# Softmax shares multiplied into the probability rows in place, in the attention stream of a four-layer kernel

## The reference

```
scores = einsum('bhqd,bhkd->bhqk', q, k) / sqrt(32)      # k, v: image key first, then 512 words
scores = where(kj <= qi + 1, scores, -10000.0) + mask
attn = softmax(scores, axis=-1)
out = einsum('bhqk,bhkd->bhqd', attn, v).transpose(0, 2, 1, 3).reshape(B, S, 512) @ c_proj_w + c_proj_b
x = x + out
```

## Time and profile before

| | |
|---|---|
| median of 3 runs | 4083.1 us (4080.97 to 4084.29) |
| the profiled execution, its own time | 4085.57 us |
| its span in the trace | 4083.9 us |
| TensorE busy | 3902.9 us (96%) |
| VectorE busy | 2336.8 us (57%) |
| ScalarE busy | 1064.0 us (26%) |
| attention stream | from 3059 us of the span to its end |

### The profile page before, as it was taken

How to read it: one execution, slowest core, us unless ns; L and a number is a source line. 1 busy time by engine, 2 the same in 40 slices (tenths; PEclk the granted TensorE clock), 3 DMA queues, 4 the chain that set the end, 5 groups by cost and what they waited for, 6 DMA issues and landing times. The chain is left out here.

```text
span 4083.9 us, 170825 instructions
## 1 busy us (share of the span) xinstructions
PE 3902.9 (96%) x77684; PEld 2648.1 (65%) x77684; DVE 2336.8 (57%) x8378; ACT 1064.0 (26%) x3931; POOL 158.9 (4%) x373
## 2 busy tenths in 40 slices
PE   6799999999999999999999999998679999999998
PEld 4577777777666666678887777765435555555555
DVE  3565655666566566556556655665326656666564
ACT  1111111111111111111111111111005555555554
POOL 0000000000000000000000000000000000000000
PEclk9999999999999999999999999999969999999999
DMA  5000000000000000000000000001000000000000
GB/s 187 3 4 4 3 3 3 3 4 3 3 3 3 4 3 3 3 4 3 3 4 3 3 3 3 3 3 64 2 6 1 14 11 9 11 12 14 11 6 19
DMA packets 34256, 46.75 MB, mean 11 GB/s; under 512 B 5820, under 2 KB 22252, under 8 KB 33527
## 3 DMA queue, kind: packets, MB, share of 16 engines
q1 hardware_dynamic: 31222, 29.43, 2.3%
q10 hardware_dynamic: 2304, 6.29, 0.4%
HBM read 27.33 MB, written 8.39 MB: 9 GB/s over the span
## 5 line engine op out<-in xcount | busy, mean ns | idle before, releaser
L201 PE MATMUL bank<-wh,h 128*16 128x256 f32 (+1 forms) x17408 | 1002.7, 370 | 52.6 <-ACT h L237 50.8
L181 PE MATMUL bank<-wh,h 128*8 128x256 f32 x16384 | 991.0, 381 | 62.2 <-DVE h L356 31.3
L201 PEld LDWEIGHTS bank<-wh,h 128*16 128x16 f32 (+1 forms) x17408 | 540.1, 97 | 333.9 <-ACT h L237 75.6
L181 PEld LDWEIGHTS bank<-wh,h 128*8 128x8 f32 x16384 | 482.4, 90 | 379.0 <-DVE h L356 50.2
L328 DVE STREAM_TRANSPOSE tp<-bank 128x256 f32<-128x256 f32 x512 | 230.4, 450 | 644.1 <-PE bank L181 644.1
L187 PE MATMUL bank<-wh,h 128*8 128x128 f32 x16384 | 550.9, 274 | 0.0
L187 PEld LDWEIGHTS bank<-wh,h 128*8 128x8 f32 x16384 | 455.6, 90 | 106.2 <-issue 2.5
L250 ACT ACTIVATE gates_sb<-pre_sb 128x32 f32<-128x32 f32 x512 | 117.5, 230 | 1357.6 <-DVE pre_sb L330 1357.6
L225 PE MATMUL bank<-stage,w_qkv 128*32 128x128 f32 x11904 | 386.4, 273 | 0.0
L225 PEld LDWEIGHTS bank<-stage,w_qkv 128*32 128x32 f32 x11904 | 344.3, 110 | 42.6
L237 ACT ACTIVATE h<-sum 128x64 f32<-128x64 f32 (+1 forms) x544 | 137.8, 253 | 786.9 <-DVE sum L272 786.9
(11 more groups left out here) (131 smaller groups left out, 3346.8 us busy)
## 6 DMA issues: line engine op xcount, KB each, us to landing
xrows<-in_x_dram SPq DMA_DIRECT2D x32, 256.0 KB, 3.8
out_dram<-X SPq DMA_DIRECT2D x32, 256.0 KB, 2.6
w_qkv<-in_L_cond_c_attn_w_dram SPq DMA_DIRECT2D x1, 3072.0 KB, 17.7
wh<-in_L_cond_w_W_dram ACTq DMA_DIRECT2D x4, 512.0 KB, 8.5
w_qkv<-in_L_cond_w_W_dram ACTq DMA_DIRECT2D x4, 512.0 KB, 10.3
wx<-in_L_cond_Wx_dram SPq DMA_DIRECT2D x2, 1024.0 KB, 8.3
wh<-in_L_cond_Wh_dram SPq DMA_DIRECT2D x2, 1024.0 KB, 10.5
mask_all<-in_mask_Bx1x1xS_ff_dram SPq DMA_DIRECT2D x8, 256.0 KB, 3.3
```

The lines of the kernel that those rows point to most:

```text
L181: mm = pe.matmul(mem.ps0[32 * j:32 * j + B, 0:2 * P], h0[:, us, k, ts, :], columns_of(mem.wh0[:, k, 0:3:2, :], j), start=(k == 0), stop=(k ...
L201: mm = pe.matmul(mem.ps12[32 * j:32 * j + B * len(ls), P * l0:P * l1], h12[:, us, k, ts, l0:l1, :].rearrange("p l b -> p (l b)"), columns_ ...
```

## The change

The probability rows themselves are multiplied by their share, in place, by VectorE, before TensorE turns them. `shares` has one number for each row and head (it was spread to 128 columns). The extras (image and hidden weights) are multiplied by the share too. TensorE no longer turns the shares, ScalarE no longer copies them, and VectorE copies bank 7 where it multiplied it. A new signal, `probs_ready`, stands between VectorE's last multiplication and TensorE's first transpose of the unit.

```diff
                     if r <= qc:
                         if r == 0:
-                            pe.wait_ge(s.exps_done, HPG * (v + 1))
+                            pe.wait_ge(s.probs_ready, v + 1)
...
                     else:
-                        pe.wait_ge(s.sums_ready, v + 1)
-                        pe.wait_ge(s.extras_in, v + 1)
-                        pe.transpose(bank[:, P:2 * P], mem.shares[:, v % RING, :], mem.ident[:, :])
                         mm = pe.matmul(bank[FAR * qc:FAR * qc + EXTRAS * HPG, 0:P],
...
-                        if qc == 0 and v >= 2 * QC:
-                            act.wait_ge(s.weighed_kept, v // QC - 1)
                         rows = slice(FAR * qc, FAR * qc + EXTRAS * HPG)
-                        nc.scalar.copy(mem.probs_extra[rows, :], bank[rows, 0:P])
...
-                        nc.scalar.copy(mem.shareT[:, v // QC % 2, qc * P:(qc + 1) * P],
-                                       bank[:, P:2 * P]).then_inc(s.turn_kept, 1)
+                        nc.scalar.copy(mem.probs_extra[rows, :], bank[rows, 0:P]).then_inc(s.turn_kept, 1)
...
                 dve.wait_ge(s.sums_full, i + 1)
-                nc.vector.reciprocal(mem.shares[:, slot, :].rearrange("p (g c) -> p g c", g=HPG),
-                                     mem.sums[:, slot, :].unsqueeze(2).to_broadcast([P, HPG, HD])).then_inc(s.sums_ready, 1)
+                nc.vector.reciprocal(mem.shares[:, slot, :], mem.sums[:, slot, :]).then_inc(s.sums_ready, 1)
+                dve.wait_ge(s.sums_ready, i + 1)
+                dve.wait_ge(s.extras_in, i + 1)
+                nc.vector.tensor_tensor(mem.extras[:, slot, :].rearrange("p (g e) -> p g e", e=EXTRAS),
+                                        mem.extras[:, slot, :].rearrange("p (g e) -> p g e", e=EXTRAS),
+                                        mem.shares[:, slot, :].unsqueeze(2).to_broadcast([P, HPG, EXTRAS]), ALU.mult)
+                for g in range(HPG):
+                    row = mem.probs[qc][:, g, 1:]
+                    ins = nc.vector.tensor_scalar(row, row, mem.shares[:, slot, g:g + 1], None, ALU.mult)
+                ins.then_inc(s.probs_ready, 1)
...
                     dve.wait_ge(s.weighed, i - 2)
-                    dve.wait_ge(s.turn_kept, ended[i - 2])
-                    nc.vector.tensor_tensor(mem.attnT[hg // HG % 2][:, hg % HG, :], mem.banks[7][:, :],
-                                            mem.shareT[:, hg % 2, :], ALU.mult).then_inc(s.weighed_kept, 1)
+                    nc.vector.tensor_copy(mem.attnT[hg // HG % 2][:, hg % HG, :], mem.banks[7][:, :]).then_inc(s.weighed_kept, 1)
...
-        mem.shares = sb(ctx, "shares", [P, RING, P])
-        mem.shareT = sb(ctx, "shareT", [P, 2, T])
+        mem.shares = sb(ctx, "shares", [P, RING, HPG])
```

More of the change, by code:

```diff
@@ L1135, in __init__ @@
         self.sums_ready = new("sums_ready")
+        self.probs_ready = new("probs_ready")
         self.weighed = new("weighed")
```

## The result

The changed kernel takes 4164.73 us (median of 4 runs, 4162.82 to 4172.67) against 4082.03 us before in the same comparison: ratio 1.0204, interval 1.0188 to 1.0220, slower by 83 us. The forecast was 4148 us with a range of 4106 to 4197.

The account below looks back on a forecast made before the run. TensorE was taken to bound the kernel, busy 198.56 of 200 us. Terms -30 + 14 + 16 + 33 + 20 + 12 = +65 us gave a median of 4148 us, 8-in-10 range 4106 to 4197.

Parts of the forecast that it names:

- Bound and mechanism: TensorE bounds the stream; its first transposes would wait for VectorE's sums and multiplications, which stand behind a kept product.
- The removal: On TensorE, 128 transposes of the shares at 0.235 us each go: -30 us.
- I read 0.195 as 0.067 plus 0.13 fixed: VectorE's in-place multiplications: 0.195 us apart at 128 columns, 0.067 for columns plus 0.13 fixed; 0.395 at 512.
- full length: Rival: VectorE's multiplication runs at 1.04 ns a column, 0.60 us at 512; +117 us, 4200 us; chance 0.13.
- no surcharge: Rival: VectorE's multiplication issues at 0.01 us plus half a ns a column; +21 us, 4104 us; chance 0.08.
- errata table: Skill-page estimate for VectorE's multiplication: 58 cycles and half the columns at 0.96 GHz, 0.33 us for 512; sum +47 us.
- The chain: Time from start of `sums_of` to release of TensorE's first transpose: 2.28 us for qc = 3, 2.02 for qc = 2.
- the release of TensorE: Time taken for releasing TensorE behind VectorE's multiplications: 0.08 us.
- The stalls: TensorE's waits before first transposes: 0.62 us 23 times, 2.35 us 7 times, 1.22 us 27 times, plus 20 us at the ends.
- jobless steps: About 12 steps of first and last sequence without a job between; stalls of 1.3 to 2.3 us each, 20 us.
- The clock: Granted clock dips after the 7 longest TensorE stalls, 1.7 us lost each: 12 us; none charged to shorter stalls.
- The clock rival: Rival: TensorE stalls of 1.22 us also bring a clock dip, 46 us more, 4194 us; chance 0.12.

Follow-up runs that it names:

- the load alone: Changed kernel with multiplications writing to a spare tile, TensorE turning unmultiplied rows once the exponentials are done; 4060.23 us against 4080.6 for the kernel before.
- the removals alone: Changed kernel without the extras' and rows' multiplications and without the wait for them; 4055.41 us against 4080.6 for the kernel before.

## Why the prediction was right, and what was mis-sized

**Bound and mechanism.** Right. TensorE bounds the stream, and `probs_ready` stands behind a kept product. A wait there costs 31 us even without the new work, the load alone nothing measurable.

**The removal.** -30 us forecast, -25 to -27 measured (3.40 us a sequence). At `l % 4 = 3` it gave 0.37 and not 0.26 us, as the rows of before (weigh, shares, extras) and after show:

```profile
4000.74 0.43 PE L813 MATMUL bank<-probsT,v 128*32 128x128 f32 x8
4001.09 0.33 PE L789 MATMUL bank<-ident,shares 128*128 128x128 f32 x1
4001.36 0.39 PE L790 MATMUL bank<-ident,extras 128*8 128x128 f32 x2
```

```profile
3727.57 0.43 PE L810 MATMUL bank<-probsT,v 128*32 128x128 f32 x8
3727.82 0.38 PE L787 MATMUL bank<-ident,extras 128*8 128x128 f32 x2
```

From L813 to the extras 4001.36 - 4000.74 = 0.62 us before, 0.25 after. TensorE thus arrives sooner at that wait, which makes the wait longer and the step no shorter. Elsewhere it gave less: the steps of the run with the removals alone are shorter by 0.11 us at `l % 4` = 0 and 2, 0.25 at 1 and 0.37 at 3. The distance from one start to the next, from which the term was taken, was a fair mean and wrong for each place.

**The price of a multiplication.** The step "I read 0.195 as 0.067 plus 0.13 fixed" held: from 281 ns at 128 columns the length grows by 0.52 ns a column, and four of 512 take 1.67 us, (1.67 - 0.48) / 3 = 0.397 from one to the next for a forecast 0.395. The rivals of full length and of no surcharge fall with it. The Trainium skill, page "VectorE: DVE Perf Modes", section "The perf-mode tier table", has the two elements a cycle that this slope shows; the estimate of 0.33 us for 512 columns by its errata table was short by 0.07. With a constant for the scalar it is (1.43 - 0.42) / 3 = 0.337 us, so what the figure lacked here is the price of the scalar from a row. The 0.13 us fixed are thus 0.06 for the scalar, as the rows of L919 and L922 had it, and 0.07 that the multiplications have with a constant too.

**The chain.** 2.28 and 2.02 us forecast, 2.36 and 2.09 measured. It is the release of TensorE that was too short: at `l = 11` the multiplications end at 3564.54 + 1.40 = 3565.94, and the transposes start 0.14 us later, for 0.08 taken.

**The stalls.** 83 us forecast, 90.4 measured as waits. At `l % 4 = 3` 1.22 forecast, 1.33 to 1.40 measured (0.07 from the chain, 0.11 from the larger removal); at `l` = 4, 8, 12 0.62 against 2.36 - (1.87 - 0.11) = 0.60, with 0.53 shown as a wait, where an error of 0.08 in the chain and one of 0.10 in the removal cancel; at `l = 0` 2.35 against 2.36 to 2.43. The places of `l % 4 = 3` are 28 and not 27. Waits of 1.33, 0.53 and 2.36 us at 28, 23 and 7 places are 66 us; the other 24 us, where 20 was forecast, stand in ten waits at the start of the stream and in the jobless steps. An even sequence comes to 6.28 us where the sum had 4 x 1.22 + 3 x 0.62 + 2.35 - 3.76 = 5.3.

**The clock** was the term most off. I charged 12 us to the seven `l = 0` waits. The windows give instead, as length times what lies under the clock of before, about 813 x 0.02 = 16 us in the middle and 172 x 0.10 = 17 in the last sequence of the profiled execution; of the latter some 12 show in the length, since TensorE's busy time rose there by 147.10 - 138.87 = 8.2 us though about 3.4 of work went; the rest must have fallen into waits.

Dips came at steps of several kinds, and not at every `l = 0`. The clock rival (a dip at each 1.2 us wait) did not hold either: of the 24 waits of 1.33 us in the six middle sequences five have a dip behind them. Filling the waits took 22 us off and these five dips away, which puts them down to the idle TensorE; the run with a constant, which waits 1.09 us at the same places, has none there. For the dips at `l` = 1 and 2 that is not shown, and why five of 24 waits bring one stays open; the places are counted in one profiled execution of each kernel. The median execution is 8 us shorter than the profiled one, with a mean granted clock of 0.977 for 0.974, so it should hold fewer dips.

In all, 83 us is 18 over the forecast sum: some 8 from waits, 3 to 5 from the smaller removal, the rest, 5 to 7, from the clock. The mechanism was right, and the terms that were too small are the clock and the stalls.

## What to carry to other kernels

A multiplication on an engine that is idle 40% of the time can still cost nearly its full length, when another engine's next step waits for it; price the distance between the two, not the load. Look first at what stands ahead of the new work in its own engine's list: here one kept product, and moving the sums ahead of it gave back 70 of 83 us. Signal each piece that the waiting engine can start on; a signal for the whole cost 60 us.

## What was not expected of the hardware

- A `TENSOR_SCALAR` with a constant has 0.137 us from one to the next at 128 columns, 0.07 over its columns; with a scalar from a row 0.195, in place or not. The same constant form lasts 170 ns at 128 columns behind a reciprocal of 128 columns, 196 behind one of 4, and 220 behind multiplications.
- A 128x128 transpose between products of other shapes is worth from 0.11 to 0.37 us, by what stands beside it.
- Unneeded TensorE work in its waits made the kernel 22 us faster, with the granted clock of the last sequence at 0.97 instead of 0.87.
